# Folding tiles, transposes and Hadamard products of the first block behind each third's value products, with stores one unit behind

## The chip, the core and the metric

The kernel runs on one core of one Trainium2 chip. The metric is the device time of one execution in microseconds (us). Engines are called by the profile's names: PE is TensorE (PEld its weight loads), DVE is VectorE, ACT is ScalarE, POOL is GpSimd, SP is SyncE, which here only issues transfers.

## What is computed

One transformer block, 4 batches of 1024 rows of 512 numbers, all in float32. A layer norm with a modulation (six rows made from a small conditioning input) feeds causal attention with 16 query heads of 32 and one shared key and value head. The gated result is added to the rows. A second layer norm and modulation feeds a gated network of 2048: 

```
x_ug = fwht(h * SU_ug) / 64;  u = x_ug @ W_up.T * s_up;  g = x_ug @ W_gate.T * s_gate
y = fwht(silu(g) * u * SU_dp) / 64;  out = x + gate * (y @ W_down.T * s_dp)
```

`fwht` is a normalised Walsh-Hadamard transform. The kernel does not transform `silu(g) * u`. It folds the 2048-long transform into W_down once, on the chip, and it transforms the 512-long input of each block of 512 rows by two crossing stages on DVE and a 128x128 Hadamard product on PE.

## The kernel before

**Two phases.** Attention walks over 64 heads H (16 per batch). The network then walks over 8 blocks of 512 rows with 16 steps each. "Left" is 64 - H, so head 59 has 5 left. Under attention lies side work that the network needs at its start: the folding of W_down, and the layer norm, transposes, crossing and Hadamard products of the first block.

**Units and thirds.** A head has 9 units (`NU`). In unit u PE makes one bank of scores (`score`, L1365), then runs the side work of that unit (`side_step(units[u])`), and after units 2, 5 and 8 it multiplies one third of the probabilities by the values (`weigh`, L1386, 10 matmuls): after unit 2 the last third of the head before, after 5 and 8 the first two thirds of this head. The main loop is at L1416 to L1423. ACT takes the exponential of each score bank (L754), copies the finished output banks out (`evacuate`, L738, after the exponential of units 2 and 5), and then does its part of the unit's side work. POOL zeroes the triangles of units 0, 1, 2, 7 and 8 (L806).

**Side work and its ring.** The regular side work of unit i is slot i of the row maxima of head H + 2: a product on PE into a side bank (`max_slot`, L1223) and a reduction on DVE (`reduce_slot`, L827 and L830). In unit 1 comes also the transpose of the negated maxima of head H + 1 (`max_top`, L1230, which waits for `negate_maxima` on DVE, L840). The side work shares three PSUM banks as a ring. `side_places` numbers all pieces in the order in which PE takes them, piece n uses bank n mod 3, and PE may write a bank only when the piece three places earlier has been read (`side_slot` waits for `side_free`). Query products of four heads (24 matmuls, L1175) come at the begin of heads with H mod 4 = 1, and output tiles of the batch before in heads with H mod 16 = 3, 4 and 5.

**Folding.** There are 16 "across" tiles (`fold_raw` in, L1250, two float32 matmul entries) and then 16 "along" tiles (`fold_again` in, L1255, two matmuls). For each one, PE fills a side bank. ACT waits for it, issues the load of the tile after next, waits until the store of the tile before last has landed (`fold_out`, two buffers), and writes the rounded half (`fold_halves`, L649). DVE writes the rest and frees the bank (`fold_rest`, L920). ACT issues the 512 KB store `STORE_AFTER` units later, behind the other work of that unit, after waiting for DVE (`store_fold`, L637). The list `FOLDS` says which heads and units have a tile: before, mostly units 3, 5 and 7 of a head, and 4 and 7 of the heads with 15 and 14 left.

**The first block.** SP loads its rows (1 MB, L442) and the first weights (0.5 MB, L447) when `BLOCK_IN` heads are left. DVE takes statistics (`STAT_LEFT`), ACT the square root, which switches its table twice (L671, `NORM_LEFT`), DVE the rows (L938). Four transposing pieces (`turn`, L1261) are freed by ACT. DVE crosses in two stages (`cross`, L950 and L951), ACT and DVE split the outcome (`round_crossed`, L676, `crossed_rest`, L960), and four Hadamard pieces follow (`had_tile`, L1267).

Of the kernel before, what the change touches and what calls it, by code (L numbers as in the profile page):

```python
# [12 lines left out]
KT = D // P  # L13
HEADS = 16
# [53 lines left out]

FOLDS = [("across", left, u) for left in (19, 18, 17, 16) for u in (3, 5, 7)] + [("across", left, u) for left in (15, 14) for u in (4, 7)]
FOLDS += [("along", left, u) for left in (10, 9, 8) for u in (3, 5, 7)] + [("along", 7, 7)]
FOLDS += [("along", left, u) for left in (6, 5) for u in (3, 5, 7)]
BLOCK_IN, STAT_LEFT, NORM_LEFT, TURN_LEFT, CROSS_LEFT, HAD_LEFT = 6, 5, 4, 3, 2, 1
TURN_UNITS, HAD_UNITS = (2, 4, 6, 8), (1, 2, 3, 4)

# [4 lines left out]
TAIL_TILES = {3: 0, 4: 1, 5: 2, 8: 3, 9: 4, 10: 5, 13: 6, 14: 7}  # L83
NT = HALF // P
UG_RING, D_RING = 3, 4
STORE_AFTER, LOAD_BEFORE = 2, 1


def side_work(H, heads):

    b, n = divmod(H, HEADS)
    left = heads - H
    begin, units = [], [[] for _ in range(NU)]
    if n % 4 == 1 and H + 3 < heads:
        begin = [("q", (H + 3) // 4, h) for h in range(2)]
    if H + 1 < heads:
        units[TOP_UNIT].append(("top", H + 1))
    if H + AHEAD < heads:
        for i in range(NS):
            units[i].append(("max", H + AHEAD, i))  # L100
    if b:
        for u, t in OUT_TILES.get(n, {}).items():
            units[u].append(("out", b - 1, t))
    if H - n + HEADS < heads:
        for u in range(NU):
            if (n, u) in ROWS:
                units[u].append(("rows", b + 1, *ROWS[n, u]))
        if n == KV_STEP:
            units[1].append(("kv", b + 1, 0))
            units[4].append(("kv", b + 1, 1))  # L110
            units[7].append(("v", b + 1))
    for kind in ("across", "along"):
        for i, (_, at, u) in enumerate(f for f in FOLDS if f[0] == kind):
            if at == left:
                units[u].append((kind, i))
    for k in range(KT):
        if left == TURN_LEFT:
            units[TURN_UNITS[k]].append(("turn", k))
        if left == HAD_LEFT:
            units[HAD_UNITS[k]].append(("had", k))  # L120
    return begin, units


def side_before():
# [7 lines left out]
def side_places(B):  # L132

    order = side_before()
    for H in range(B * HEADS):
        begin, units = side_work(H, B * HEADS)
        order += begin + [key for unit in units for key in unit]
    return {key: place for place, key in enumerate(order)}


# [127 lines left out]
def phase(nc, io, dram, B, S, sem, banks, K, A, W, F):  # L268
# [98 lines left out]
    with nc.Block() as block:  # L367

        @block.sync
        def _(sp):  # L370
# [109 lines left out]

            def step(H):
                b, n = divmod(H, HEADS)
                begin, _ = side_work(H, ALL)
                for key in begin:
                    side_taken(sp, key)
                if H + 3 < ALL:
                    load_stack(H + 3)
                if H + 1 < ALL:
                    load_max(H + 1)
                if begin and begin[0][1] + 1 < ALL // 4:  # L490
                    fetch_group(begin[0][1] + 1)
                if H:
                    gather(H - 1)
                if b and n == 2:
                    load_gains(b - 1)
                    load_residual(b - 1, 0)
                    load_residual(b - 1, 1)
                tiles = OUT_TILES.get(n, {}) if b else {}
                for u, t in tiles.items():
                    if u < INVERT_UNIT:  # L500
                        store_tile(b - 1, t)
                if H and H % 4 == 0:
                    spread_inverses(H // 4 - 1)
                for u, t in tiles.items():
                    if u >= INVERT_UNIT:
                        store_tile(b - 1, t)
                if b == 0 and 1 <= n <= TT // 2 and B > 1:
                    for t in (2 * n - 2, 2 * n - 1):
                        load_rows(1, t)
                if n > KV_STEP - 1 and b + 2 < B:  # L510
                    for t in (2 * (n - KV_STEP), 2 * (n - KV_STEP) + 1):
                        load_rows(b + 2, t)
                left = ALL - H
                if left == BLOCK_IN:
                    load_block(0)
                    load_upgate(0)
                if left == CROSS_LEFT:
                    for i in range(NS - SLOTS_SIDE, NS):
                        side_taken(sp, ("max", ALL - 1, i))
                    load_upgate(1)  # L520
# [63 lines left out]
        def _(act):  # L584
# [159 lines left out]

            def step(H):
                b, n = divmod(H, HEADS)
                begin, units = side_work(H, ALL)
                side_step(begin)
                for u in range(NU):
                    at = H * NU + u  # L750
# [6 lines left out]
                    if u == 2 * THIRD - 1:  # L757
                        evacuate(H, 0)
                    side_step(units[u])
                    if b + 1 < B:  # L760
                        if (n, u) == (ROOT_STEP, 0):
                            layer_norm_deviations(nc, act, T, eps, b + 1)
                        if (n, u) in NORM_ROWS:
                            layer_norm_rows(nc, act, T, b + 1, NORM_ROWS[n, u])
# [3 lines left out]
                    left = ALL - H  # L768
                    if (left, u) == (NORM_LEFT, 0):
                        deviations(0)  # L770
                    if left == CROSS_LEFT and u >= NU - KT:
                        round_crossed(0, (u - NU + KT,))
                    if (left, u) == (HAD_LEFT, 5):
                        cast_upgate(0)

            act.wait_ge(c_in, 16)
# [34 lines left out]
        def _(dve):  # L811
# [251 lines left out]

            def step(H):
                b, n = divmod(H, HEADS)
                begin, units = side_work(H, ALL)
                side_step(begin)
                for u in range(NU):
                    side_step(units[u])
                    if H and H % 4 == 0 and u == INVERT_UNIT:  # L1070
                        invert_sums(H // 4 - 1)
                    if H > 4 and H % 4 == 1 and u in (1, 3):
# [14 lines left out]
                        block_inverses(0)  # L1087
                    if left == NORM_LEFT and 4 <= u < 4 + NT:
                        block_rows(0, u - 4)
                    if left == CROSS_LEFT and u in (0, 2):  # L1090
                        cross(0, u // 2)
                    if left == CROSS_LEFT and u in (6, 8):
                        crossed_rest(0, (u - 6, u - 5))
                    if (left, u) == (HAD_LEFT, 7):
                        split_upgate(0)

            def split(hi, lo, raw):
# [66 lines left out]
        def _(pe):  # L1164
# [249 lines left out]
            modulation((3, 4))  # L1414
            side_step(before[to_max:])
            for H in range(ALL):  # L1416
                begin, units = side_work(H, ALL)
                side_step(begin)
                for u in range(NU):
                    score(H, u)  # L1420
                    side_step(units[u])
                    if u % THIRD == THIRD - 1 and (H or u >= THIRD):
                        weigh(*divmod(H * THIRD + u // THIRD - 1, THIRD))  # L1423
            weigh(ALL - 1, THIRD - 1)
            for g in range(STEPS):
                up_gate(g)
# [48 lines left out]
```

## Time and profile before

| | us |
|---|---|
| median of 3 runs | 2136.5 |
| lowest and highest run | 2133.1, 2136.51 |
| the profiled execution's own time | 2139.19 |
| its span | 2137.5 |
| PE busy in the span | 2018.9 (94%) |
| DVE, ACT, POOL busy | 1205.8, 788.3, 169.6 |

The profile is of one execution, 2.7 us above the median. Its span leaves out 1.7 us around the first and last instruction. Attention's heads run from about 87 to 1033 us, the network from there to the end. The granted TensorE clock was 0.978 of full on average.

### The profile page before, as it was taken

To read this page: it belongs to the slowest core of one execution; us is meant where nothing else is said; L and a number is where in the kernel's file an instruction comes from. 1 tells how busy PE (TensorE), PEld (TensorE's weight loads), DVE (VectorE), ACT (ScalarE), POOL (GpSimd) and SP (SyncE) were. 2 spreads that over 40 slices of the span, in tenths; PEclk is the share of its full clock that TensorE was granted. 3 is DMA by queue.
4 is the path that set the end of the run, shared out by engine and by line. 5 is a ranking of instruction groups with operands and counts; after the bars stand their busy time and mean duration, and the time that the engine had idled before them with its cause. 6 is when DMAs were issued, how large, how long until landed. Compare 5 with 4: busy or idle time off the path is not lost.

```text
span 2137.5 us, 27288 instructions
## 1 busy us (share of the span) xinstructions
PE 2018.9 (94%) x9584; PEld 1526.7 (71%) x9584; DVE 1205.8 (56%) x2607; ACT 788.3 (37%) x1323; POOL 169.6 (8%) x522
## 2 busy tenths in 40 slices
PE   6999999999999889877999999999999999999998
PEld 5665667666666556544688888888888888888887
DVE  5677676776677556556445544555445554455433
ACT  2156553655456443445422222222222222222211
POOL 0021121111112111112000000000000000000000
PEclk9799999999999999998999999999999999999999
DMA  7143244224333465563534533534335343343441
GB/s 242 41 133 77 54 125 119 73 69 116 109 99 71 118 200 157 179 220 94 178 132 138 195 127 119 177 119 167 121 127 171 124 160 127 128 162 126 146 137 60
DMA packets 113663, 279.87 MB, mean 131 GB/s; under 512 B 27755, under 2 KB 33131, under 8 KB 113401
## 3 DMA queue, kind: packets, MB, share of 16 engines
q1 hardware_dynamic: 104168, 248.71, 37.9%
q10 hardware_dynamic: 9360, 29.43, 4.1%
q8 instruction: 77, 1.26, 0.2%
q14 instruction: 58, 0.47, 0.1%
HBM read 199.15 MB, written 35.93 MB: 110 GB/s over the span
## 4 chain that ended last, share of the span: by engine, by line
PE 54%; DMA 2%; DVE 1%; ACT 1%; issue 1%; SPq 0%; POOL 0%; ACTq 0%; DVEq 0%; POOLq 0%
PE banks L1175 33%; PE banks L1325 16%; PE banks L1386 2%; DMA down_split_dram<-fold_split 1%; PE banks L1261 1%; PE banks L1267 1%; PE banks L1365 1%; PE banks L1223 0%; DVE masked_scores L827 0%; PE banks L1255 0%; ACT fold_split L649 0%; DVE fold_split L920 0%; POOL probs L806 0%; DMA o_group<-o_raw 0%; ACT probs L754 0%
## 5 line engine op out<-in xcount | busy, mean ns | idle before, releaser
L1175 PE MATMUL banks<-h_t_split,w_ring 128*128 128x512 f32 x3072 | 718.9, 390 | 2.6 <-DVE w_ring L968 2.6
L1175 PEld LDWEIGHTS banks<-h_t_split,w_ring 128*128 128x128 f32 x3072 | 577.7, 188 | 123.2 <-DVE w_ring L968 3.0
L693 ACT ACTIVATE silu_gate<-banks,scale_upgate 128x512 f32<-128x512 f32 x128 | 88.3, 690 | 803.0 <-PE banks L1175 803.0
L754 ACT ACTIVATE probs<-banks 128x512 f32<-128x512 f32 x576 | 318.7, 597 | 153.2 <-PE banks L1365 151.4
L1325 PE MATMUL banks<-d_ring,y_split 128*128 128x512 f32 x1536 | 370.6, 390 | 0.1
L976 DVE SCALAR_TENSOR_TENSOR y<-banks,scale_upgate,silu_gate 128x512 f32<-128x512 f32 x128 | 95.9, 749 | 433.4 <-ACT silu_gate L693 433.4
L1325 PEld LDWEIGHTS banks<-d_ring,y_split 128*128 128x128 f32 x1536 | 287.2, 188 | 59.6 <-DVE y_split L982 0.5
L1386 PE MATMUL banks<-probs,v_ones 128*64 128x128 f32 (+3 forms) x1920 | 304.4, 448 | 3.9 <-POOL probs L806 3.9
L1223 PE MATMUL banks<-k_stack,q_stacks 96*128 96x512 f32 (+3 forms) x768 | 251.7, 372 | 17.0 <-DVE q_split L848 11.2
L1386 PEld LDWEIGHTS banks<-probs,v_ones 128*64 128x64 f32 x1920 | 149.1, 140 | 162.1 <-issue 130.2
L1365 PE MATMUL banks<-q_stacks,k_stack 98*128 98x512 f32 (+3 forms) x768 | 263.4, 386 | 0.1
L806 POOL TENSOR_SCALAR_AFFINE_SELECT probs<-probs 128x128 f32<-128x128 f32 x512 | 167.3, 346 | 861.0 <-ACT probs L754 859.9
L830 DVE TENSOR_REDUCE max_all<-banks 128x1 f32<-128x512 f32 x256 | 172.3, 686 | 81.2 <-PE banks L1223 80.7
L1365 PEld LDWEIGHTS banks<-q_stacks,k_stack 98*128 98x128 f32 x768 | 144.6, 194 | 52.1 <-issue 34.5
L1223 PEld LDWEIGHTS banks<-k_stack,q_stacks 96*128 96x128 f32 x768 | 145.8, 198 | 46.2 <-DVE q_split L848 14.8
L968 DVE TENSOR_TENSOR w_ring<-upgate_raw,w_ring 128x1024 fp32r<-128x1024 f32 x128 | 155.9, 1218 | 15.8 <-ACT w_ring L685 15.5
L827 DVE CUSTOM_DVE_ANT_0 masked_scores<-banks,mask_row,max_all 128x512 f32<-128x512 f32 (+3 forms) x256 | 137.0, 546 | 19.1 <-PE banks L1223 12.8
L685 ACT ACTIVATE w_ring<-upgate_raw 128x1024 fp32r<-128x1024 f32 x128 | 135.1, 1056 | 8.2 <-DMA upgate_raw<-in_w_ug 8.2
L827 DVE CUSTOM_DVE_ANT_0 masked_scores<-banks,mask_row 128x512 f32<-128x512 f32 (+3 forms) x256 | 121.4, 483 | 12.1 <-PE banks L1223 6.6
L738 ACT ACTIVATE o_raw<-banks 128x512 f32<-128x512 f32 x128 | 76.5, 598 | 127.8 <-PE banks L1386 127.0
L1175 PE MATMUL banks<-ow_split,o_split 128*128 128x512 f32 x384 | 94.4, 394 | 2.7 <-DVE max_all L827 1.7
L1175 PE MATMUL banks<-h_t_split,qw_group 128*128 128x512 f32 x384 | 92.4, 396 | 0.0
(117 smaller groups left out, 1283.8 us busy)
## 6 DMA issues: line engine op xcount, KB each, us to landing
upgate_raw<-in_w_ug SPq DMA_DIRECT2D x128, 512.0 KB, 4.1
d_ring<-down_split_dram SPq DMA_DIRECT2D x128, 512.0 KB, 3.3
q_stacks<-q_split SPq DMA_DIRECT2D x192, 128.0 KB, 2.4
o_group<-o_raw SPq DMA_DIRECT2D x128, 128.0 KB, 2.3
x<-in_x SPq DMA_DIRECT2D x32, 256.0 KB, 3.0
o_group<-inverse_sums_dram SPq DMA_DIRECT2D x64, 128.0 KB, 2.6
x_and_residual<-in_x SPq DMA_DIRECT2D x32, 256.0 KB, 3.2
x_dram<-x_and_residual SPq DMA_DIRECT2D x32, 256.0 KB, 2.5
```

The source lines that it names most:

```text
L685: nc.scalar.activation(wr[g % 2][:, 0], ugr[g % UG_RING][:], ACT.Copy).then_inc(ug_cast, 1)
L754: nc.scalar.activation(pr[:, u, :], score_bank[:, at % SLOTS_SCORE, :], ACT.Exp, scale=SCALE).then_inc(exped, 1)
L806: last = nc.gpsimd.affine_select(out=triangle, in_=triangle, compare_op=ALU.is_ge, fill=0.0, base=0, pattern=[[1, P]], channel_multiplier=-1)
L827: last = nc.vector.tensor_tensor_reduce(out=masked_scores[:, i % 2, col:col + w], in0=part, in1=mask[:, HALF - w:HALF], scale=1.0, scalar= ...
L830: last = nc.vector.tensor_reduce(out, part, AX.X, ALU.max)
L968: nc.vector.tensor_tensor(wr[g % 2][:, 1], ugr[g % UG_RING][:], wr[g % 2][:, 0].bitcast(F32), ALU.subtract).then_inc(ug_ready, 1)
L976: nc.vector.scalar_tensor_tensor(out=y[:], in0=up_bank[:, s, :], scalar=sug[:, 0, f:f + 1], in1=sg[:, s, :], op0=ALU.mult, op1=ALU.mult).t ...
L1175: ins = nc.tensor.matmul(out, weights(a, k), moving(m, k), start=(k == 0 and a + m == 0), stop=(last and k == kts - 1 and a == 1))
L1223: last = nc.tensor.matmul(side[:, r, col:col + w], qst[0:96, s, qt * P:(qt + 1) * P], kst[0:96, b % 2, k0:k0 + w], start=True, stop=True)
L1325: last = nc.tensor.matmul(acc[:, t, :], ys[s][:, a, t * P:(t + 1) * P], dr[g % D_RING][:, m, :], start=(f == 0 and a + m == 0), stop=(f == ...
L1365: last = nc.tensor.matmul(score_bank[:, at % SLOTS_SCORE, col:col + w], kst[0:98, b % 2, kt * P:(kt + 1) * P], qst[0:98, s, q0:q0 + w], st ...
L1386: last = nc.tensor.matmul(obank[half * 2 * HD:(half + 1) * 2 * HD, c, q0 - c * HALF:q0 - c * HALF + w], vs[:, b % 2, kt, :], pr[:, u, col: ...
```

## The change

Folding tiles, transposes and Hadamard pieces move from `units` to a new list `ends`, which PE runs after the unit's value products, and ACT and DVE after the unit's other side work. All stand in units 2, 5 or 8. Across tiles: three per head with 19 to 15 left, one with 14. Along tiles: three per head with 12 to 8 left, one with 7. Before, the along tiles stood with 10 to 5 left. The store of a tile comes one unit behind it, not two. The first block's load comes with 7 heads left (6 before), the statistics with 6 (5), the square root and rows with 5 (4), the four transposes with 4 (three) and 3 (one), where all four stood with 3 left. The crossing comes with 3 left in units 4 and 6 (2 left, units 0 and 2), the rounding in unit 8 as one piece, the rest of the splitting with 2 left in units 0 and 1, and the Hadamard pieces with 2 left (three) and 1 left (one), where all four stood with 1 left.

```diff
--- before.py
+++ after.py
@@ -68,11 +68,11 @@
 
 
 
-FOLDS = [("across", left, u) for left in (19, 18, 17, 16) for u in (3, 5, 7)] + [("across", left, u) for left in (15, 14) for u in (4, 7)]
-FOLDS += [("along", left, u) for left in (10, 9, 8) for u in (3, 5, 7)] + [("along", 7, 7)]
-FOLDS += [("along", left, u) for left in (6, 5) for u in (3, 5, 7)]
-BLOCK_IN, STAT_LEFT, NORM_LEFT, TURN_LEFT, CROSS_LEFT, HAD_LEFT = 6, 5, 4, 3, 2, 1
-TURN_UNITS, HAD_UNITS = (2, 4, 6, 8), (1, 2, 3, 4)
+
+FOLDS = [("across", left, u) for left in (19, 18, 17, 16, 15) for u in (2, 5, 8)] + [("across", 14, 2)]
+FOLDS += [("along", left, u) for left in (12, 11, 10, 9, 8) for u in (2, 5, 8)] + [("along", 7, 2)]
+BLOCK_IN, STAT_LEFT, NORM_LEFT, CROSS_LEFT, CAST_LEFT = 7, 6, 5, 3, 1
+TURNS, HADS = [(4, 2), (4, 5), (4, 8), (3, 2)], [(2, 2), (2, 5), (2, 8), (1, 2)]
 
 
 
@@ -83,14 +83,14 @@
 TAIL_TILES = {3: 0, 4: 1, 5: 2, 8: 3, 9: 4, 10: 5, 13: 6, 14: 7}
 NT = HALF // P
 UG_RING, D_RING = 3, 4
-STORE_AFTER, LOAD_BEFORE = 2, 1
+STORE_AFTER, LOAD_BEFORE = 1, 1
 
 
 def side_work(H, heads):
 
     b, n = divmod(H, HEADS)
     left = heads - H
-    begin, units = [], [[] for _ in range(NU)]
+    begin, units, ends = [], [[] for _ in range(NU)], [[] for _ in range(NU)]
     if n % 4 == 1 and H + 3 < heads:
         begin = [("q", (H + 3) // 4, h) for h in range(2)]
     if H + 1 < heads:
@@ -112,13 +112,12 @@
     for kind in ("across", "along"):
         for i, (_, at, u) in enumerate(f for f in FOLDS if f[0] == kind):
             if at == left:
-                units[u].append((kind, i))
-    for k in range(KT):
-        if left == TURN_LEFT:
-            units[TURN_UNITS[k]].append(("turn", k))
-        if left == HAD_LEFT:
-            units[HAD_UNITS[k]].append(("had", k))
-    return begin, units
+                ends[u].append((kind, i))
+    for kind, where in (("turn", TURNS), ("had", HADS)):
+        for k, (at, u) in enumerate(where):
+            if at == left:
+                ends[u].append((kind, k))
+    return begin, units, ends
 
 
 def side_before():
@@ -133,8 +132,8 @@
 
     order = side_before()
     for H in range(B * HEADS):
-        begin, units = side_work(H, B * HEADS)
-        order += begin + [key for unit in units for key in unit]
+        begin, units, ends = side_work(H, B * HEADS)
+        order += begin + [key for u in range(NU) for key in units[u] + ends[u]]
     return {key: place for place, key in enumerate(order)}
 
 
@@ -480,7 +479,7 @@
 
             def step(H):
                 b, n = divmod(H, HEADS)
-                begin, _ = side_work(H, ALL)
+                begin, _, _ = side_work(H, ALL)
                 for key in begin:
                     side_taken(sp, key)
                 if H + 3 < ALL:
@@ -744,7 +743,7 @@
 
             def step(H):
                 b, n = divmod(H, HEADS)
-                begin, units = side_work(H, ALL)
+                begin, units, ends = side_work(H, ALL)
                 side_step(begin)
                 for u in range(NU):
                     at = H * NU + u
@@ -757,6 +756,7 @@
                     if u == 2 * THIRD - 1:
                         evacuate(H, 0)
                     side_step(units[u])
+                    side_step(ends[u])
                     if b + 1 < B:
                         if (n, u) == (ROOT_STEP, 0):
                             layer_norm_deviations(nc, act, T, eps, b + 1)
@@ -768,9 +768,9 @@
                     left = ALL - H
                     if (left, u) == (NORM_LEFT, 0):
                         deviations(0)
-                    if left == CROSS_LEFT and u >= NU - KT:
-                        round_crossed(0, (u - NU + KT,))
-                    if (left, u) == (HAD_LEFT, 5):
+                    if left == CROSS_LEFT and u == NU - 1:
+                        round_crossed(0, range(KT))
+                    if (left, u) == (CAST_LEFT, 5):
                         cast_upgate(0)
 
             act.wait_ge(c_in, 16)
@@ -1063,10 +1063,11 @@
 
             def step(H):
                 b, n = divmod(H, HEADS)
-                begin, units = side_work(H, ALL)
+                begin, units, ends = side_work(H, ALL)
                 side_step(begin)
                 for u in range(NU):
                     side_step(units[u])
+                    side_step(ends[u])
                     if H and H % 4 == 0 and u == INVERT_UNIT:
                         invert_sums(H // 4 - 1)
                     if H > 4 and H % 4 == 1 and u in (1, 3):
@@ -1087,11 +1088,11 @@
                         block_inverses(0)
                     if left == NORM_LEFT and 4 <= u < 4 + NT:
                         block_rows(0, u - 4)
-                    if left == CROSS_LEFT and u in (0, 2):
-                        cross(0, u // 2)
-                    if left == CROSS_LEFT and u in (6, 8):
-                        crossed_rest(0, (u - 6, u - 5))
-                    if (left, u) == (HAD_LEFT, 7):
+                    if left == CROSS_LEFT and u in (4, 6):
+                        cross(0, u // 2 - 2)
+                    if left == CROSS_LEFT - 1 and u in (0, 1):
+                        crossed_rest(0, (2 * u, 2 * u + 1))
+                    if (left, u) == (CAST_LEFT, 7):
                         split_upgate(0)
 
             def split(hi, lo, raw):
@@ -1414,13 +1415,14 @@
             modulation((3, 4))
             side_step(before[to_max:])
             for H in range(ALL):
-                begin, units = side_work(H, ALL)
+                begin, units, ends = side_work(H, ALL)
                 side_step(begin)
                 for u in range(NU):
                     score(H, u)
                     side_step(units[u])
                     if u % THIRD == THIRD - 1 and (H or u >= THIRD):
                         weigh(*divmod(H * THIRD + u // THIRD - 1, THIRD))
+                    side_step(ends[u])
             weigh(ALL - 1, THIRD - 1)
             for g in range(STEPS):
                 up_gate(g)
```

## Rows read from the trace of the kernel before

**Rows 1.** The page: the group that zeroes triangles (busy, mean ns | idle before)

```profile
L806 POOL TENSOR_SCALAR_AFFINE_SELECT probs<-probs 128x128 f32<-128x128 f32 x512 | 167.3, 346 | 861.0 <-ACT probs L754 859.9
```

**Rows 2.** Stages by windows: from:to, length, busy time of five engines, clock, DMA share, GB/s

```profile
720.40:815.20 94.80, 81.57 (x387) 48.33 (x385) 60.11 (x163) 49.08 (x95) 15.08 (x48) 0.98 0.60 184
...
834.00:875.10 41.10, 39.99 (x202) 29.03 (x199) 23.78 (x61) 13.48 (x26) 5.99 (x16) 1.00 0.44 127
...
875.10:981.10 106.00, 79.71 (x389) 50.31 (x387) 61.28 (x168) 50.04 (x94) 14.32 (x48) 0.92 0.66 211
...
955.40:981.10 25.70, 14.45 (x64) 8.83 (x62) 12.15 (x34) 9.42 (x17) 2.70 (x10) 0.80 0.57 195
...
981.10:1032.90 51.80, 43.93 (x231) 26.89 (x230) 32.28 (x75) 34.71 (x65) 14.03 (x32) 0.90 0.22 60
...
992.00:1009.10 17.10, 14.13 (x73) 9.31 (x71) 11.98 (x38) 8.86 (x16) 2.67 (x8) 0.80 0.18 48
```

**Rows 3.** Windows of heads 13, 13 to 14, 13 to 16, 14 to 15, and of 49 and 57

```profile
264.00:274.50 10.50, 9.75 (x57) 6.18 (x55) 8.64 (x22) 6.54 (x13) 2.46 (x8) 1.00 0.60 155
264.00:284.80 20.80, 19.58 (x112) 12.37 (x110) 16.95 (x48) 13.41 (x27) 4.92 (x16) 1.00 0.52 135
264.00:309.90 45.90, 44.59 (x245) 29.45 (x244) 32.22 (x98) 25.84 (x52) 9.34 (x32) 1.00 0.44 117
274.50:294.70 20.20, 19.63 (x112) 12.41 (x110) 15.42 (x51) 12.79 (x26) 4.67 (x16) 1.00 0.45 123
790.50:802.80 12.30, 11.55 (x61) 6.99 (x60) 9.67 (x23) 7.71 (x15) 2.47 (x8) 1.00 0.71 224
929.70:941.00 11.30, 10.47 (x59) 6.59 (x57) 9.28 (x23) 7.21 (x14) 2.69 (x8) 1.00 0.55 145
```

**Rows 4.** Waits from 720.4 to 1032.9 us: total, times, longest

```profile
PE banks L1230 <- DVE neg_max L840: 22.6, 11, 8.9
...
ACT fold_split L649 <- DMA down_split_dram<-fold_split: 18.7, 4, 9.2
...
PE banks L1255 <- DVE fold_split L920: 10.4, 10, 1.1
...
PE banks L1250 <- DVE fold_split L920: 7.1, 8, 1.0
...
PE banks L1386 <- POOL probs L806: 3.9, 2, 2.5
```

**Rows 5.** Timeline of head 54, engines PE, ACT and DVE, around its first two tiles

```profile
879.71 0.64 PE L1255 MATMUL banks<-fold_again,hadamard 128*128 128x512 f32 x2
...
880.42 0.39 PE L1223 MATMUL banks<-k_stack,q_stacks 96*128 96x512 f32 x1
880.65 0.40 PE L1365 MATMUL banks<-q_stacks,k_stack 98*128 98x512 f32 x1
...
880.76 0.69 ACT L649 ACTIVATE fold_split<-banks,signs 128x512 fp32r<-128x512 f32 x1 [0.41 <-PE banks L1255]
...
881.48 0.75 DVE L920 SCALAR_TENSOR_TENSOR fold_split<-banks,signs,fold_split 128x512 fp32r<-128x512 f32 x1 [0.88 <-ACT fold_split L649]
...
882.38 0.70 PE L1255 MATMUL banks<-fold_again,hadamard 128*128 128x512 f32 x2 [1.09 <-DVE fold_split L920]
```

**Rows 6.** Waits of PE in head 57, which begins behind query products

```profile
PE banks L1223 <- DVE q_split L848: 0.7, 1, 0.7
```

**Rows 7.** Timeline of head 62, DVE and POOL, during the crossing

```profile
1010.82 1.31 DVE L951 TENSOR_TENSOR x_normed<-h_t 128x1024 f32<-128x1024 f32 x1
...
1011.35 4.11 POOL L806 TENSOR_SCALAR_AFFINE_SELECT probs<-probs 128x128 f32<-128x128 f32 x4 [0.29 <-ACT probs L754]
```

**Rows 8.** Timeline of head 46, PE, and a window over heads 47 and 48

```profile
738.13 0.28 PE L1230 MATMUL banks<-ident,neg_max 128*16 128x128 f32 x1 [1.39 <-DVE neg_max L840]
...
739.46 2.83 PE L1386 MATMUL banks<-probs,v_ones 128*64 128x512 f32 x10
...
753.50:790.50 37.00, 31.20 (x148) 19.14 (x147) 20.18 (x60) 16.49 (x32) 4.98 (x18) 1.00 0.62 195
```

## The prediction, made blind

> **What bounds the kernel now.** I first read the page: PE is busy for 94% of the span, so only its idle time, or time at the lower clock, can be won, and only under the heads that carry the moved work. Its line on the triangles [rows 1] is needed further below. Then I cut that stretch into stages [rows 2]. The six heads with across tiles (45 to 50) take 94.8 us, heads 52 and 53, still without tiles, 41.1, the heads with along tiles (54 to 59) 106.0, the last four 51.8. Against that stand heads without side work of this kind [rows 3]: a head costs 10.5 us where H mod 4 is 1, 10.3 where it is 2 (20.8 less 10.5), and four successive heads cost 45.9, one of them being followed by 24 query matmuls.
>
> The waits say what fills the difference [rows 4]. Three kinds matter. PE waits 22.6 us before the transpose of the maxima, because DVE is late. DVE is late because it sits behind ACT, and ACT waits 18.7 us for stores of along tiles to land, once for 9.2. That once is head 59: a store queued together with the block's 1 MB load and the 0.5 MB weight load. The head takes 25.7 us at a granted clock of 0.80 [rows 2]. Third, PE waits 17.5 us (10.4 + 7.1, 18 times) directly for DVE to free a side bank [rows 4].
>
> That third wait is the one to understand. In head 54 the first tile starts on PE at 879.71, ACT rounds it from 880.76, DVE frees the bank from 881.48 + 0.75, and the next tile, three places on in the ring, starts at 882.38 after 1.09 idle [rows 5]. In between PE had four products, 0.23 us apart (880.42 to 880.65). With tiles in units 4 and 7, as in head 49, value products stood between a tile and the piece that reuses its bank, and no such wait occurs.
>
> **The change part by part.**
>
> *PE's own work* is the same, only elsewhere. Head 49 with two across tiles takes 12.3 us against 10.5, so a tile costs 0.9. Head 57 with one along tile takes 11.3 against 10.5, so 0.8 [rows 3].
>
> *The store's wait goes.* Before, tile 1 of a head (unit 3) was stored behind unit 5's work and its buffer wanted in unit 7. Now tile (unit 2) is stored in unit 3 and its buffer wanted in unit 8, five units later with two thirds of value products in between. I cost this wait at nothing. The cover is two thirds of a head of 10 us and more [rows 3]. If a store in a jam still takes longer, ACT stands there, the exponentials behind it too, and PE after them; the price is what it is now, up to 9.2 a time. The traffic grows by an estimate from 211 GB/s [rows 2] to some 240 in heads 54 to 56 (nine tiles with two transfers of 0.52 MB each in about 50 us, and the rest as now), which I take as carried.
>
> *The block's load* now comes with 7 left, when the last along tile is just done. No store is awaited behind it until the Hadamard pieces, four heads later. The jam of head 59 goes. DVE's statistics need the load a head later, as before.
>
> *The ring wait stays, and there is one more per head.* Behind a tile at unit 2 or 5 now come score, max, score, max, score, then the max piece of the same bank: five products, none of them a value product. They give one more 0.23 us of cover than before. I take 0.9 - 0.2 = 0.7 for an across tile (7.1 / 8 = 0.9 now) and 1.0 - 0.2 = 0.8 for an along tile (10.4 / 10 now) [rows 4]. Behind a tile at unit 8 come score, max, score, the small transpose, then max slot 1: three products and a little, so 0.2 more than now: 1.1 and 1.25. A query product in the same position, without the load that ACT issues ahead of rounding, already costs 0.7 [rows 6]. After heads 48, 52 and 56 the query products lie in between and cover it. The bounds: nothing, if DVE's and ACT's part overlaps better than I think, and 1.4 us each, if DVE is late as well.
>
> *Sum for the across heads.* Heads 45 to 50 without tiles: 45.9 + 20.8 = 66.7. Sixteen tiles: 14.4. Eleven waits at units 2 and 5: 7.7. Four at unit 8: 4.4. Together 93.2 against 94.8: -1.6.
>
> *Sum for the along heads.* Heads 52 and 53 41.1, four heads 45.9, heads 58 and 59 20.2 [rows 3]: 107.2. Sixteen tiles 12.8, eleven waits 8.8, three at unit 8 3.8, and 1.0 for the square root's two table switches on ACT in head 59 (a guess between 0 and 3 from the head that has them now: 10.9 us, 981.1 to 992.0, against 20.2 - 10.3 = 9.9). Together 133.6 against 41.1 + 106.0 = 147.1: -13.5. Here lies the gain, and nearly all of it is in the old heads 58 and 59. Heads 52 and 53 themselves get some 9 us longer.
>
> *The last four heads.* Head 60 gets three transposing pieces, four short transposes each: I take 0.4 a piece, half an along tile (bounds 0 and 0.8), so +1.3. Head 61 (17.1 us) gives three of them up but gains the crossing: DVE's 12.0 busy us there [rows 2], less an estimated 1.6 (two normalising rows and the inversion of the sums, which leave it), plus four crossing operations of 1.2 to 1.3 (1.31 in [rows 7]) make 15.5, so DVE will bound it at about 16: -1.1. Heads 62 and 63 lose PE's wait for POOL (2.5 of the 3.9 in [rows 4]) and, of the time that the low clock costs the last four heads (51.8 us at 0.90 [rows 2], so some 5 us granted at half), I take 0.8: -3.3. Together -3.1. The bounds are -6 and +3.
>
> Here a row speaks against the change. During the crossing four triangle operations on POOL took 4.11 us [rows 7], where one takes 0.346 on average [rows 1]. The crossing's second stage now stands in unit 6, just ahead of the triangles of units 7 and 8, which PE waits for in the next head. The Trainium skill, "GPSIMD Engine Reference", section "1. Specifications", says that GpSimd shares its SBUF interfaces with VectorE and contends with VectorE instructions that have two SBUF inputs, as the crossing has. By that rule the 2.5 us move to another place rather than vanish, and the last four heads give -0.6 in place of -3.1.
>
> *The total* is -1.6 - 13.5 - 3.1 = -18.2. I add back 2 for one or two further stretches at the lower clock, since a third of the value products took 2.83 us behind an idle 1.39 [rows 8], of which the low clock is half, 1.4: -16. From the profiled execution's 2139.2 that gives 2123, and the median of the runs shown lies 2.7 lower: 2121 rounded.
>
> **The rivals.**
>
> *Slower: the clock falls.* Each tile now leaves a ring wait of 0.7 to 1.3 us, 29 in all against 18. If PE falls to 1.2 GHz behind such waits, each costs 1.4 us more in the next value products. From twelve of them on, the gain of 16 is gone. With twenty it is +12: 2148. For it speaks the 1.39 idle of head 46 with the half-speed third behind it. Against it, heads 47 and 48 had four of the eight waits of L1250 [rows 4] and kept a clock of 1.00 [rows 8]. The Trainium skill, "TensorE: Matmul & The Clock Gate", section "A second HAM failure mode: psum-queue depth-cycling", says that frequent short idles between groups of matmuls, as PE cycles through PSUM banks, make the clock swing between its two levels. That is this rival, and the row of heads 47 and 48 does not bear it out. Chance 0.13.
>
> *Much faster: the ring does not bind.* If the bank is free in time behind the value products, the 24.7 us of ring waits in the two sums fall away: 2096. For it, ACT has its copies done and waits for the tile alone. Against it, the order of places gives the same bank after only five products. Chance 0.12.
>
> *About the same: the jam moves.* The denser along heads or the block's load with the last store make DVE or PE wait elsewhere, for 9 us as in head 59, and POOL keeps its 2.5 us: -16 + 12 = -4, 2132. It would show as a DMA wait above 5 us in heads 52 to 58. Chance 0.15.
>
> The stores might also be issued no earlier than before, since ACT waits for DVE there. That would leave the other 9.5 us of ACT's waits for along stores (18.7 less 9.2) and is inside the forecast's range.
>
> **How the numbers follow.** The forecast's own case, 0.60, runs from 2108 to 2130. The range reaches to the third rival and the near part of the first and leaves out the far ends: 2105 to 2138. About 0.2% (4.3 us) is what a measurement of this kernel can tell from no change. Faster by more: the forecast's case, the ring rival and a small part of the third, 0.76. Within it: 0.11. Slower: 0.13.
>
> **What would show each step.** No wait of ACT L649 on a store above 1 us. Head 59 below 12 us. PE waiting for L920 ahead of L1223, not ahead of L1250 and L1255, some 29 times for 20 to 30 us. Heads 52 and 53 together near 50. Head 61 near 16 with DVE busy almost throughout. The prediction is wrong if PE's waits for L920 vanish, or if more than three new stretches at the lower clock appear between 720 and 980.

## The result and the profile after

The changed kernel takes 2117.4 us (median of 4 runs, 2113.1 to 2118.6) against 2136.5: a ratio of 0.991, with an interval of 0.9893 to 0.9928. The forecast was 2121, with a range of 2105 to 2138. The profiled execution has a span of 2115.3 us against 2137.5. Line numbers of the changed kernel are one off in places (scores L1366, row maxima L1224, value products L1387).

Windows of the changed kernel over the same heads as in [rows 2]: heads 45 to 50, 52 and 53, 54 to 59, 59, 60 to 63, 61, 62. The columns are those of [rows 2].

```profile
720.80:812.50 91.70, 81.11 (x388) 48.28 (x386) 58.66 (x162) 49.85 (x95) 14.03 (x48) 1.00 0.63 197
831.60:880.20 48.60, 43.90 (x214) 31.36 (x212) 27.10 (x66) 17.34 (x31) 5.97 (x16) 1.00 0.71 229
880.20:964.10 83.90, 72.43 (x375) 46.40 (x374) 58.78 (x169) 49.81 (x92) 13.48 (x48) 0.98 0.64 201
951.10:964.10 13.00, 11.06 (x57) 6.79 (x55) 10.15 (x36) 8.83 (x15) 2.19 (x8) 0.87 0.20 44
964.10:1013.10 49.00, 41.99 (x232) 26.00 (x230) 29.57 (x70) 32.55 (x62) 11.23 (x32) 0.93 0.21 51
975.90:988.00 12.10, 10.44 (x62) 6.57 (x60) 10.43 (x24) 7.23 (x14) 2.71 (x8) 1.00 0.26 67
988.00:1002.90 14.90, 11.42 (x51) 6.77 (x50) 8.85 (x19) 10.14 (x20) 4.12 (x8) 0.77 0.22 56
```

Set against [rows 2] this gives most of the account. The heads with along tiles, and the two before them that now carry tiles too, take 132.5 us in place of 147.1. The across heads gain 3.1, the last four 2.8. Head 59 alone falls from 25.7 to 13.0. Together that is 20.5 of the 22.2 us between the two spans. Some 2.3 us more lie in the network's part, which the change does not touch, and the other heads took about 0.6 longer. Waits of the changed kernel over the same stretch (total, times, longest):

```profile
ACT fold_split L648 <- PE banks L1251: 18.7, 16, 2.1
PE banks L1224 <- DVE fold_split L920: 16.8, 26, 1.1
ACT fold_split L648 <- PE banks L1256: 13.1, 15, 2.4
PE banks L1231 <- DVE neg_max L840: 7.5, 6, 3.5
...
PE banks L1176 <- DVE fold_split L920: 2.9, 3, 1.0
...
PE banks L1387 <- POOL probs L806: 1.2, 1, 1.2
```

No line with ACT waiting for a store is left, where [rows 4] have 18.7 us for the along tiles. PE's wait for the negated maxima is down from 22.6 to 7.5. But PE now waits for DVE's fold_split 29 times (26 + 3), 19.7 us in all, where it waited 18 times and 17.5 us. These waits stand ahead of row maxima and output tiles, no longer ahead of the folding tiles.

The timeline of head 54 of the changed kernel shows one of them, for comparison with [rows 5]: PE first, then ACT and DVE.

```profile
884.82 0.73 PE L1256 MATMUL banks<-fold_again,hadamard 128*128 128x512 f32 x2
...
886.33 0.40 PE L1366 MATMUL banks<-q_stacks,k_stack 98*128 98x512 f32 x1
887.48 0.51 PE L1224 MATMUL banks<-k_stack,q_stacks 96*128 96x512 f32 x1 [0.76 <-DVE fold_split L920]
...
885.96 0.69 ACT L648 ACTIVATE fold_split<-banks,signs 128x512 fp32r<-128x512 f32 x1 [0.41 <-PE banks L1256]
...
886.68 0.75 DVE L920 SCALAR_TENSOR_TENSOR fold_split<-banks,signs,fold_split 128x512 fp32r<-128x512 f32 x1 [2.50 <-ACT fold_split L648]
```

From the tile's start to the bank's reuse it takes 2.66 us (884.82 to 887.48), as before (879.71 to 882.38). PE has five products to fill it with in place of four, so 0.76 us stay where it was 1.09.

### The profile page after: what moved, and what is told of

It reads as the page before. It is cut to its first block, busy times and chain, and to the rows that moved or that the text cites. A ratio compares the mean times of both kernels' runs of the same rounds, so it can differ in the third digit from the quotient of the medians.

```text
span 2115.3 us, 27288 instructions
## 1 busy us (share of the span) xinstructions
PE 2012.7 (95%) x9584; PEld 1524.0 (72%) x9584; DVE 1202.9 (57%) x2607; ACT 790.0 (37%) x1323; POOL 164.8 (8%) x522
## 4 chain that ended last, share of the span: by engine, by line
PE 52%; DVE 1%; DMA 0%; ACT 0%; issue 0%; SPq 0%; POOL 0%; POOLq 0%; DVEq 0%; ACTq 0%
PE banks L1176 33%; PE banks L1326 16%; PE banks L1268 1%; PE banks L1262 1%; PE banks L1387 0%; DMA inverse_sums_dram<-sums 0%; PE banks L1366 0%; DVE out_sb L1003 0%; DMA o_group<-inverse_sums_dram 0%; DVE out_sb L994 0%; ACT probs L753 0%; DMA o_group<-o_raw 0%; PE banks L1237 0%; DVE masked_scores L827 0%; DVE o_group L886 0%
## 5 line engine op out<-in xcount | busy, mean ns | idle before, releaser
L1387 PE MATMUL banks<-probs,v_ones 128*64 128x128 f32 (+3 forms) x1920 | 300.0, 443 | 1.2 <-POOL probs L806 1.2
L1224 PE MATMUL banks<-k_stack,q_stacks 96*128 96x512 f32 (+3 forms) x768 | 251.7, 372 | 34.5 <-DVE fold_split L920 16.8
L1366 PE MATMUL banks<-q_stacks,k_stack 98*128 98x512 f32 (+3 forms) x768 | 259.9, 382 | 0.0
L1387 PEld LDWEIGHTS banks<-probs,v_ones 128*64 128x64 f32 x1920 | 147.5, 139 | 153.7 <-issue 125.3
L806 POOL TENSOR_SCALAR_AFFINE_SELECT probs<-probs 128x128 f32<-128x128 f32 x512 | 162.5, 336 | 845.9 <-ACT probs L753 844.5
L1224 PEld LDWEIGHTS banks<-k_stack,q_stacks 96*128 96x128 f32 x768 | 144.5, 196 | 73.8 <-DVE fold_split L920 24.5
L1366 PEld LDWEIGHTS banks<-q_stacks,k_stack 98*128 98x128 f32 x768 | 142.6, 193 | 44.0 <-issue 27.1
L968 DVE TENSOR_TENSOR w_ring<-upgate_raw,w_ring 128x1024 fp32r<-128x1024 f32 x128 | 156.0, 1218 | 17.5 <-ACT w_ring L684 17.2
L1176 PE MATMUL banks<-ow_split,o_split 128*128 128x512 f32 x384 | 94.8, 396 | 5.7 <-DVE fold_split L920 2.9
```

What stands on the lines that cost most here:

```text
L806: last = nc.gpsimd.affine_select(out=triangle, in_=triangle, compare_op=ALU.is_ge, fill=0.0, base=0, pattern=[[1, P]], channel_multiplier=-1)
L968: nc.vector.tensor_tensor(wr[g % 2][:, 1], ugr[g % UG_RING][:], wr[g % 2][:, 0].bitcast(F32), ALU.subtract).then_inc(ug_ready, 1)
L1176: ins = nc.tensor.matmul(out, weights(a, k), moving(m, k), start=(k == 0 and a + m == 0), stop=(last and k == kts - 1 and a == 1))
L1224: last = nc.tensor.matmul(side[:, r, col:col + w], qst[0:96, s, qt * P:(qt + 1) * P], kst[0:96, b % 2, k0:k0 + w], start=True, stop=True)
L1366: last = nc.tensor.matmul(score_bank[:, at % SLOTS_SCORE, col:col + w], kst[0:98, b % 2, kt * P:(kt + 1) * P], qst[0:98, s, q0:q0 + w], st ...
L1387: last = nc.tensor.matmul(obank[half * 2 * HD:(half + 1) * 2 * HD, c, q0 - c * HALF:q0 - c * HALF + w], vs[:, b % 2, kt, :], pr[:, u, col: ...
```

## The experiments

Each is compared with the kernel before, run beside it in the same batch. The text gives the median, then its ratio to the kernel before, with the 95% interval in brackets. The medians of the kernel before in the three batches were 2135.4, 2137.8 and 2136.9 us. The changed kernel was not run in these batches, so it is compared by its ratio, 0.991.

**One part at a time, on the kernel before.** Three runs take one part of the change each. First the store:

```diff
-STORE_AFTER, LOAD_BEFORE = 2, 1
+STORE_AFTER, LOAD_BEFORE = 1, 1
```

> The kernel before, with nothing changed but the store of a folding tile one unit behind it instead of two. Theory (the gain is stores that land in time): ACT's waits for stores (27.8 us before: 18.7 along, 9.1 across) fall below 5 us in all, and the 9.2 us jam under head 59 goes too, since that store is issued just ahead of the block's load; 2120 to 2128 us. PE's direct waits for DVE's fold_split stay at 17 to 18 us. Rival (the gain comes from standing behind the value products): within 3 us of the kernel before, 2134 to 2139.

Measured: 2119.3 us, 0.9922 [0.9902 to 0.9941]. One number gives 16 us of the 19. The waits of this kernel:

```profile
PE banks L1255 <- DVE fold_split L920: 9.0, 9, 1.1
...
PE banks L1230 <- DVE neg_max L840: 7.6, 9, 3.4
PE banks L1250 <- DVE fold_split L920: 7.1, 8, 1.0
...
ACT fold_split L649 <- DMA down_split_dram<-fold_split: 1.4, 3, 0.9
```

ACT's waits for stores are gone but for 1.4 us, and with them 15 us of PE's wait for the maxima (22.6 before), while the ring waits stay (16.1). I had expected the jam under heads 58 and 59 to go too. It has not gone from the queues, and the two heads still take 31.8 us, where they took 40.1. Their windows, first the two together in the kernel before, then 58 and 59 in this one:

```profile
941.00:981.10 40.10, 26.08 (x125) 16.09 (x123) 21.63 (x61) 17.17 (x32) 5.11 (x17) 0.87 0.64 211
...
929.10:943.40 14.30, 11.72 (x64) 7.28 (x61) 9.69 (x28) 8.89 (x17) 1.95 (x7) 1.00 0.79 249
943.40:960.90 17.50, 13.45 (x63) 8.14 (x61) 11.67 (x34) 8.26 (x16) 2.73 (x10) 0.90 0.87 293
```

The DMA share reaches 0.87, and the three stores issued from 936.4 to 943.9 took 6.0 to 9.8 us to land. Issued a unit earlier, they have nearly landed when their buffers are wanted (ACT waits 1.4 us in all). The one in the jam before had taken 11.4.

Then the along tiles alone, two heads earlier, in the old units and with the old stores:

```diff
-... for left in (10, 9, 8) for u in (3, 5, 7)] + [("along", 7, 7)]
-... for left in (6, 5) for u in (3, 5, 7)]
+... for left in (12, 11, 10) for u in (3, 5, 7)] + [("along", 9, 7)]
+... for left in (8, 7) for u in (3, 5, 7)]
```

> The kernel before, with nothing changed but the along tiles two heads earlier (12 to 7 left in place of 10 to 5), so that the block's load at 6 left meets no store. Theory: heads 58 and 59 lose 16 us together, heads 52 and 53 gain 9 or so in waits and tiles but heads that lose theirs give as much back; in all 10 to 14 us faster than before, 2122 to 2127. The short waits for stores (three tiles a head, 2 to 3 us each) stay. Rival (placing behind value products, or the store's unit, is the gain): within 4 us of the kernel before.

Measured: 2125.0 us, 0.9946 [0.9929 to 0.9962]. Heads 58 and 59 fall from 40.1 to 20.2 us (first line below). The other waits for stores are still there, and those of the along tiles have grown, from 9.5 us outside the jam (18.7 less 9.2) to 14.2:

```profile
947.40:967.60 20.20, 19.74 (x114) 12.45 (x111) 16.37 (x51) 12.79 (x26) 4.64 (x16) 1.00 0.62 174
...
ACT fold_split L649 <- DMA down_split_dram<-fold_split: 14.2, 4, 4.0
PE banks L1230 <- DVE neg_max L840: 13.3, 10, 2.7
ACT fold_split L649 <- DMA down_across_dram<-fold_split: 9.0, 4, 2.4
```

Last the place behind the value products alone: units 2, 5 and 8 through `ends`, in the old heads, stores two units behind, the first block as before.

```diff
-... for u in (3, 5, 7)] ... for u in (4, 7)]        # across; along alike
+... for u in (2, 5, 8)] ... for u in (5, 8)]
-                units[u].append((kind, i))
+                ends[u].append((kind, i))
```

> The kernel before with the same heads for its folding tiles, the same stores two units behind and the same times for the first block, but the tiles behind the value products of units 2, 5 and 8. Theory: it trades waits: PE waits some 29 times for a bank (18 before), 20 to 25 us, and ACT's short waits for stores go; the jam is shortened or stays, so 2124 to 2136 us. Rival (standing behind the value products is the gain): 2115 to 2120, as the changed kernel.

Measured: 2117.5 us, 0.9914 [0.9897 to 0.993]. That is the rival's value, and my theory gave too little here. Its waits tell why (line numbers are one or two further on here):

```profile
PE banks L1225 <- DVE fold_split L921: 21.0, 28, 1.8
...
PE banks L1232 <- DVE neg_max L841: 4.2, 3, 3.4
...
ACT fold_split L649 <- DMA down_split_dram<-fold_split: 1.5, 1, 1.5
```

The ring waits are there as I expected (28 times, 21.0 us). But ACT's waits for stores go from 27.8 to 1.5 us (heads 58 and 59: 30.2 us for 40.1). I read this as the spacing: tiles three units apart, with a third of the value products between each pair, give nearly every store time to land. This run moves the place and the spacing together, so it does not separate them. Two kernels further down keep three units between tiles without standing behind the products, and ACT waits 0.4 and 2.3 us for stores there, but with the store one unit behind. That fits the spacing and does not prove it. The three parts alone give 16, 10 and 18 us and all together 19: to a large part they remove the same waits.

**The store's unit in the changed kernel.**

```diff
-STORE_AFTER, LOAD_BEFORE = 1, 1
+STORE_AFTER, LOAD_BEFORE = 2, 1
```

> The changed kernel with stores two units behind, as before. Theory (with three units between tiles the store has time either way): 2114 to 2121 us, ACT's waits for stores below 3 us. Rival (the store one unit behind is what frees the changed kernel of its store waits): 2124 us or more, with ACT waiting 10 us or more for stores.

Measured: 2119.0 us, 0.9916 [0.9899 to 0.9932], so no difference that can be told from 0.991. Among its waits is no line with ACT and a store, and fold_split's waits on PE are 16.7 + 2.9. With the new places of the tiles the store's unit is worth nothing that can be measured.

**The price of the ring.** Two kernels put something between a tile and the reuse of its bank. One has the tiles in units 1, 4 and 7:

```diff
-... for u in (2, 5, 8)] + [("across", 14, 2)]
+... for u in (1, 4, 7)] + [("across", 14, 1)]        # along alike
```

> The changed kernel, but its folding tiles in units 1, 4 and 7 of the same heads instead of 2, 5 and 8, so that value products stand between a tile and the piece that takes its bank again. Theory (29 ring waits cost the changed kernel 19.7 us): these waits fall below 5 us and the time to 2098 to 2106. Rival (the ring waits only stand where DVE or ACT would hold PE anyway): the same time as the changed kernel, 2114 to 2120, with the waits moved to L1231 or to the exponentials.

Measured: 2101.0 us, 0.9832 [0.9812 to 0.9852]. The other leaves the units and only turns the order round, on PE and on ACT:

```diff
 PE:   side_step(units[u])
+      side_step(ends[u])
       if u % THIRD == THIRD - 1 and ...: weigh(...)
-      side_step(ends[u])
 ACT:  exponential
+      side_step(ends[u])
       evacuate(...)
       side_step(units[u])
-      side_step(ends[u])
```

> The changed kernel, but the moved pieces of units 2, 5 and 8 stand ahead of the value products on PE, and ACT takes them ahead of its copy of the output banks. Nothing else moves, the ring's order included. Theory (ring waits are the price of standing behind the value products): PE's waits for fold_split fall from 19.7 to below 6 us and the time to 2099 to 2106 us, as with units 1, 4 and 7. Rival (units 1, 4 and 7 gained by their other neighbours): 2112 to 2119.

Measured: 2101.9 us, 0.9835 [0.982 to 0.985]. PE has no wait for fold_split left in either. By the ratios they are 16 to 17 us faster than the changed kernel, so of the 19.7 us of ring waits 3 to 4 come back. Part of that is seen in head 56 of the second kernel, which takes 21.6 us where the changed kernel took 19.7 (the first takes 23.4). Its window and waits:

```profile
890.40:912.00 21.60, 18.88 (x88) 12.91 (x87) 10.33 (x29) 8.64 (x16) 2.19 (x8) 0.92 0.68 219
...
DVE sums L870 <- DMA o_group<-o_raw: 3.6, 1, 3.6
...
PE banks L1176 <- DVE max_all L827: 2.5, 1, 2.5
```

DVE inverts the sums in unit 6 and waits for the gather of the head before. That gather is issued beside folding transfers and took 5.7 to 5.8 us to land, where the gathers after the last folding tile took 2.3 to 2.4. It is also wanted sooner as the heads get shorter. Behind it wait the row maxima, and PE for a bank, and a stretch at the lower clock follows (0.92 over the head).

**The crossing's place.** Crossing in head 62 and Hadamard pieces in head 63, as before, all else as changed:

```diff
-TURNS, HADS = [...], [(2, 2), (2, 5), (2, 8), (1, 2)]
+TURNS, HADS = [...], [(1, 1), (1, 2), (1, 3), (1, 4)]
-... CROSS_LEFT, CAST_LEFT = 7, 6, 5, 3, 1        # crossing in units 4 and 6
+... CROSS_LEFT, CAST_LEFT = 7, 6, 5, 2, 1        # crossing in units 0 and 2
```

> The changed kernel, but the crossing stands in head 62 (units 0 and 2), its rounding behind units 5 to 8 of it, and the Hadamard pieces in head 63, as before. Theory (the crossing in head 61 makes DVE late: 1.4 us there, 3.5 in head 62 and the low clock behind): heads 60 to 63 take 45 to 47 us in place of 48.9, in all 2 to 4 us faster, 2113 to 2116. Rival (these heads are bound by ACT and POOL once the row maxima have ended): no change or up to 2 us slower, since head 62 then waits for POOL again (2.5 us before).

Measured: 2115.3 us, 0.9898 [0.9883 to 0.9913]. The time alone can't tell this from the changed kernel. The heads can: 60 to 63 take 46.2 us in place of 48.9.

```profile
963.50:1009.70 46.20, 40.72 (x232) 25.23 (x230) 30.13 (x70) 32.42 (x62) 13.43 (x32) 0.96 0.21 53
1009.70:2115.20 1105.50, 1095.96 (x4882) 907.74 (x4880) 537.09 (x760) 278.97 (x364) 0.00 (x0) 1.00 0.43 141
```

The rival's wait is there as well: PE waits 3.5 us for POOL, where it waited 1.2. And in this profile the network's part takes 1105.5 us, against 1102.3 in the changed kernel's. PE's one wait there, for the first weights, is 3.6 us for 1.9. So what the heads gain is not seen in the span. Whether the late crossing causes that wait was not tried.

The late crossing together with tiles in units 1, 4 and 7:

> The changed kernel with folding tiles in units 1, 4 and 7 and with the crossing in head 62. Theory: the two effects add up, 2097 to 2101 us. Rival: the crossing's place is worth nothing or costs, 2101 to 2104.

Measured: 2100.6 us, 0.9825 [0.981 to 0.984]. The last four heads take 46.2 us again (49.2 with the crossing in head 61). The ratios with and without the late crossing, 0.9825 and 0.9832, are too close to separate.

**Towards a faster kernel.** The order turned round and the late crossing together:

> Folding tiles ahead of the value products (ACT's half ahead of its copy) and the crossing in head 62 with its Hadamard pieces in head 63. Theory: both effects add, heads 60 to 63 take 46 to 47 us in place of 50.0, 2097 to 2101 us, ratio 0.981 to 0.983. Rival: the crossing's place is worth nothing, 2101 to 2104.

Measured: 2098.0 us, 0.9818 [0.9805 to 0.9831], with 46.8 us for heads 60 to 63. And DVE's inversion behind the maxima:

```diff
-TOP_UNIT, INVERT_UNIT = 1, 6
+TOP_UNIT, INVERT_UNIT = 1, 8
```

> The same, and DVE inverts the sums in unit 8 of every fourth head, behind the maxima, where it did in unit 6. Theory (DVE waits there for a gather that queues behind the folding transfers, and PE then for side banks, 2.5 us in head 56): heads 54 to 57 lose some 2 us, and 1 us in all elsewhere; 2094 to 2099 us. Rival (the scaling of the group four units later then waits for the inverted sums): the same or up to 5 us slower.

Measured: 2094.3 us, 0.9802 [0.9788 to 0.9815], the lowest median of the study, 42.6 us below the kernel before. Its interval overlaps that of the kernel one step earlier, so what this step adds is read from the heads. Head 56 shows it:

```profile
888.50:905.70 17.20, 17.20 (x87) 11.78 (x86) 10.49 (x29) 8.67 (x16) 2.19 (x8) 1.00 0.76 257
```

PE is busy for all of its 17.2 us (the head takes 21.9 in the kernel one step earlier). Under heads 45 to 60 DVE waited three times for the gather, 6.6 us in all, and now waits once, 1.3 us. The first line below adds the last group's wait, 4.5 us, which comes in the network's part:

```profile
DVE sums L870 <- DMA o_group<-o_raw: 5.8, 2, 4.5
...
DVE o_group L886 <- DMA o_group<-inverse_sums_dram: 3.1, 1, 3.1
```

The second line looks like the rival's wait, DVE's scaling waiting for the inverted sums. But it too belongs to the last group, in the network's part, and it is in the kernel one step earlier (3.3 us) and in the kernel before the change (5.4 us) as well. Under the heads the rival's wait did not come. The gain in heads 54 to 57 was 4.7 us (56.7 to 52.1), twice what I had expected.

## Why the prediction was right, and where it was off

**The sums.** Forecast and measured, by the windows:

| heads | before | forecast | after |
|---|---|---|---|
| 45 to 50 | 94.8 | 93.2 | 91.7 |
| 52 to 59 | 147.1 | 133.6 | 132.5 |
| 60 to 63 | 51.8 | 48.7 | 49.0 |

**The ring wait, right in place and number.** 29 waits were forecast for 24.7 us, 29 came with 19.7. The term was mis-sized: 0.7 to 1.3 us were put on each and 0.68 measured on average. Behind a tile at unit 8 four of the seven waits are 0.97 to 1.12, a little below the forecast (1.1 and 1.25), and three are only 0.33 to 0.71. Behind one at unit 2 they are mostly 0.62 to 0.63 for across and 0.76 for along tiles, where I took 0.7 and 0.8. Behind one at unit 5 they are 0.51 and 0.62 to 0.65: there the maxima are two matmuls each, which PE spends longer on than on one, so more of the same delay is covered. The two kernels that remove the waits gain 16 to 17 us by it.

The shorter waits hide a second error. Without its 8.9 us of ring waits the stretch of heads 45 to 50 took 82.8 us, where my sum without them gives 81.1 (66.7 + 14.4). So heads and tiles were put 1.7 us too cheap there, and the two errors partly cancel in the table.

**The store's wait, right.** It was costed at nothing, and no such wait remains. Landings took 2.6 to 4.9 us, against a cover of two thirds of a head. What the step did not say is that the new places of the tiles do it alone: the store's own unit is worth nothing measurable here, though it is worth 16 us in the kernel before.

**The block's load, right.** The jam of head 59 is gone, at about the size put on it. No run moves the load alone. Moving the along tiles away from it brings heads 58 and 59 from 40.1 to 20.2 us. The two kernels that leave load and tiles in their heads and only give the stores more time bring them to 31.8 and 30.2, about half of that.

**Head 59 was put below 12 us and took 13.0.** The step that failed is the 1.0 us for the table switches. ACT's two table loads took 1.28 us each, and PE did not wait for ACT in this head. What the trace shows instead is a PE wait of 1.9 us for the negated maxima, and a clock of 0.87 over the head. The maxima come out late because DVE takes the statistics of the block in head 58: from 945.2 to 953.3 DVE works without a gap, and 3.1 us of it are the statistics. The head from which I had taken the 1.0 us (head 60 of the kernel before) has the same wait, 0.8 us, behind the statistics in its head 59. The kernel with only the along tiles moved, which also takes them in head 59, has no wait in that head and one of 1.1 us in head 60. No run moves the statistics alone.

**The last four heads, right in sum, wrong in place.** I expected head 61 to be held to 16 us by DVE. It took 12.1, and head 62 took 14.9. DVE was late about as calculated (its work for this head ran from 977.1 to 992.2, 15.1 us for the 15.5 calculated), but PE could run ahead of it until the transpose of the maxima in head 62. The step that failed is that DVE would bound head 61 within head 61: there it is busy for 10.4 of 12.1 us, and the rest falls into head 62. DVE of the changed kernel ends the crossing and the maxima only then, and PE shows what follows:

```profile
988.25 1.22 DVE L951 TENSOR_TENSOR h_t<-x_normed 128x1024 f32<-128x1024 f32 x1
...
991.98 0.17 DVE L840 SCALAR_TENSOR_TENSOR neg_max<-max_all,neg_max 128x8 fp32r<-128x8 f32 x1
...
992.20 0.38 PE L1231 MATMUL banks<-ident,neg_max 128*16 128x128 f32 x1 [3.48 <-DVE neg_max L840]
...
992.94 2.83 PE L1387 MATMUL banks<-probs,v_ones 128*64 128x512 f32 x10
```

Behind the idle 3.48 us the next third of value products runs at the lower clock again (0.77 over the head): 2.83 us, as in [rows 8]. The 2 us that I had added for the clock were not for this head in particular. The two lower stretches between 720 and 1013 us are this one and the one in head 59, and both stand in the measured columns above. Over the whole execution the mean clock rose from 0.978 to 0.986.

**POOL.** Triangles and crossing met less than feared. DVE was so late with the second stage (987.12 to 989.47) that the triangles of units 7 and 8 were done before it. They met the splitting that follows the crossing (L960, two SBUF inputs on DVE) instead:

```profile
984.74 1.03 POOL L806 TENSOR_SCALAR_AFFINE_SELECT probs<-probs 128x128 f32<-128x128 f32 x3 [5.30 <-ACT probs L753]
...
992.24 3.15 POOL L806 TENSOR_SCALAR_AFFINE_SELECT probs<-probs 128x128 f32<-128x128 f32 x5 [6.48 <-ACT probs L753]
```

The two operations beside DVE's splitting took 1.19 and 1.27 us, the three after it 0.29 each:

```profile
992.06 2.45 DVE L960 TENSOR_TENSOR h_crossed_split<-h_t,h_crossed_split 128x1024 fp32r<-128x1024 f32 x2
```

By the rule of the Trainium skill ("GPSIMD Engine Reference", section "1. Specifications") the slow ones are where DVE reads two SBUF inputs, and the trace agrees. PE did not wait for these. Of its two waits for POOL before (2.5 and 1.3 us) one of 1.2 is left, in head 63. So the 2.5 us did vanish, as the forecast had it. But as I read the trace they vanished because DVE was late with the crossing's second stage, which the forecast had not counted on, so that was luck.

**The rivals.** The clock did not fall behind the ring waits, of 1.1 us and less: heads 45 to 50 kept 1.00 with fifteen of them, heads 54 to 58 with waits of up to 1.12. The ring does bind, as forecast; the 2096 us of the rival without it come near only in the kernels that put value products between tile and reuse (2101.0 and 2101.9). The jam did not move in the changed kernel: no DMA wait of 1 us or more is among those in heads 52 to 58. A smaller wait of that kind, 3.6 us, came when the heads got shorter still, as head 56 showed.

The network's part, which the change does not touch, took 1102.3 us for 1104.6 and ranged from 1102.1 to 1105.5 over all these kernels; I count no part of it to the change. In the two profiles PE's one wait there, for the first weights, was 2.6 us before and 1.9 after, and only before was it followed by 3.4 us at the lower clock. This was not in the forecast, and the profiles' difference of 22.2 us contains it.

**The total.** The medians lie 19.1 us apart, where 15.5 were forecast (2136.5 to 2121). By the profiles it is 22.2 against 16: the three stretches gained 2.3 more than their sums, the 2 us added for the clock did not come on top, the network's part gave 2.3, and the other heads took 0.6 back. The profiles leave a miss of 6 us, the medians one of 3.6, and ring waits put too high and heads put too cheap cancel in part. That the total came so near is partly luck.

## What to carry to other kernels

A wait for a transfer can be removed by issuing it earlier, by wanting it later, or by keeping other transfers out of its way, and these gains do not add. Before counting them, see which waits each would remove. In a ring of three banks, ask what stands between a piece and the third one after it: the same tile makes no such wait where long work lies in between, and one of two thirds of a microsecond where only short work does. Once these waits are gone, look for the next one at a fixed place in the order, here DVE's inversion of sums ahead of the maxima.

## What was unexpected of the hardware

A 512 KB store landed 2.6 to 4.9 us behind its issue in the changed kernel, and 11.4 us behind it in the kernel before when it was issued after 1.5 MB of loads from another engine's queue. Three kernels have folding stores, on ACT's queue, within 9 us behind these loads on SP's: the kernel before, the one with only the earlier stores and the one with only the new places. The five such stores took 8.5 to 11.4 us, all others of these kernels 2.6 to 7.7. So here loads on one engine's queue held up stores on another's; which resource they share these runs do not show. The DMA share of that stretch reached 0.87 at 293 GB/s in the kernel with the earlier stores.

A triangle operation on POOL took 0.29 us alone and up to 1.27 us beside a DVE operation with two SBUF inputs.
